# The mixture stage of a graph layer as seven half products, with the edge sums in a stage of their own

## The reference

```
gnn: h = xn @ W.T + b;  every node its own edge too;  out[row] += deg[row]^-0.5 deg[col]^-0.5 h[col]
mix: q = xn @ Wq.T + bq (k, v alike), 16 heads of 64;  q' = relu(q P) / 8, k' alike;  kv = k'^T v
     mix = (q' kv) @ Wo.T + bo
x = x + gnn + mix
ffn: routing weights over 8 experts;  sum_e w_e * (silu(y Wg_e) * (y Wu_e)) @ Wd_e,  y = layernorm(x)
x = x + ffn
```

## Time and profile before

| | |
|---|---|
| median of 3 runs | 1088.25 us (1088.06 to 1088.41) |
| the profiled execution | 1088.11 us, its span 1086.2 us |
| granted TensorE clock, mean | 0.998 |
| PE busy | 1075.5 us, 99%, 5587 matmuls |
| DVE, ACT, POOL busy | 441.6 us, 269.9 us, 323.0 us |
| from the last h tile to the router | about 549 to 758 us of the span |

### The profile page before, as it was taken

One profiled execution on the slowest core, in us unless ns is written; L12 is line 12 of the kernel. 1 busy time (PEld: TensorE's weight loads), 2 busy tenths in 40 slices (PEclk: granted clock), 3 DMA queues, 4 the chain that ended last, 5 costly groups with the idle time before them and its releaser, 6 DMA issues.

```text
span 1086.2 us, 15078 instructions
## 1 busy us (share of the span) xinstructions
PE 1075.5 (99%) x5587; PEld 893.3 (82%) x5587; DVE 441.6 (41%) x1061; ACT 269.9 (25%) x413; POOL 323.0 (30%) x223
## 2 busy tenths in 40 slices
PE   8999999999999999999999999999999999999998
PEld 7887778887878888888878888887788888888887
DVE  6944666676641111322212123344235112314684
ACT  5320211112233345311111112434213112202221
POOL 4000011122132347400035444434208744500151
PEclk9999999999999999999999999999999999999999
DMA  7313011122244487604179987876045646205912
GB/s 269 97 30 108 13 35 54 61 70 72 70 128 127 159 296 247 209 1 155 39 196 327 307 243 205 235 218 186 1 160 189 213 179 214 66 24 221 378 66 110
DMA packets 148731, 162.36 MB, mean 149 GB/s; under 512 B 8150, under 2 KB 116018, under 8 KB 145330
## 3 DMA queue, kind: packets, MB, share of 16 engines
q1 hardware_dynamic: 148082, 159.55, 45.5%
q10 hardware_dynamic: 576, 1.84, 0.4%
HBM read 114.91 MB, written 46.45 MB: 149 GB/s over the span
## 4 chain that ended last, share of the span: by engine, by line
PE 95%; DVE 3%; issue 1%; ACT 1%; DMA 0%; ACTq 0%; DVEq 0%
PE ps L1773 10%; PE ps L1774 9%; PE ps L1775 9%; PE ps L2073 7%; PE ps L2074 7%; PE ps L2075 7%; PE ps L2014 4%; PE ps L2008 4%; PE ps L1988 3%; PE ps L1989 3%; PE ps L1939 3%; PE ps L1990 3%; PE ps L1940 3%; PE ps L1941 3%; PE ps L2131 3%; PE ps L2132 3%
## 5 line engine op out<-in xcount | busy, mean ns | idle before, releaser
L1773 PE MATMUL ps<-w_hi,xnH 128*128 128x512 f32 x464 | 184.7, 398 | 0.0
L1775 PE MATMUL ps<-w_hi,xnL 128*128 128x512 f32 x464 | 180.9, 390 | 0.0
L1774 PE MATMUL ps<-w_lo,xnH 128*128 128x512 f32 x464 | 180.8, 390 | 0.0
L827 POOL TENSOR_TENSOR acc<-acc,cw 128x320 f32<-128x320 f32 x40 | 35.7, 892 | 252.6 <-ACT cw L1028 251.4
L1773 PEld LDWEIGHTS ps<-w_hi,xnH 128*128 128x128 f32 x464 | 87.1, 188 | 18.8
L1775 PEld LDWEIGHTS ps<-w_hi,xnL 128*128 128x128 f32 x464 | 87.1, 188 | 18.6
L1774 PEld LDWEIGHTS ps<-w_lo,xnH 128*128 128x128 f32 x464 | 87.2, 188 | 17.0
L1675 DVE TENSOR_TENSOR prd<-ps,wB 128x512 f32<-128x512 f32 (+1 forms) x24 | 14.2, 592 | 142.1 <-PE ps L2075 101.2
L1939 PE MATMUL ps<-xnH,w_hi 128*128 128x512 f32 (+1 forms) x192 | 68.1, 355 | 0.0
L2073 PE MATMUL ps<-x2H,guH 128*128 128x512 f32 (+1 forms) x192 | 67.7, 352 | 0.4 <-ACT wT L1232 0.4
L2074 PE MATMUL ps<-x2L,guH 128*128 128x512 f32 (+1 forms) x192 | 67.6, 352 | 0.0
(11 more groups left out here) (421 smaller groups left out, 2127.0 us busy)
## 6 DMA issues: line engine op xcount, KB each, us to landing
cR<-c_d SPq DMA_DIRECT2D x20, 640.0 KB, 5.2
foldin<-in SPq DMA_DIRECT2D x32, 256.0 KB, 2.8
guR<-in SPq DMA_DIRECT2D x16, 512.0 KB, 5.7
w_raw<-in SPq DMA_DIRECT2D x14, 512.0 KB, 6.4
c_d<-cw SPq DMA_DIRECT2D x40, 160.0 KB
wdq<-in SPq DMA_DIRECT2D x6, 1024.0 KB, 7.3
qs0H<-qT_d SPq DMA_DIRECT2D x10, 512.0 KB, 5.2
qs0L<-qT_d SPq DMA_DIRECT2D x10, 512.0 KB, 6.5
```

Source lines behind the costliest of these rows:

```text
L1773: pe.matmul(target, xnH[:, kc, cols], wH[w][:, kc, :], start=(kc == 0), stop=False)
L1774: pe.matmul(target, xnH[:, kc, cols], wL[w][:, kc, :], start=False, stop=False)
L1775: mm = pe.matmul(target, xnL[:, kc, cols], wH[w][:, kc, :], start=False, stop=(kc == KC - 1))
```

## The change

The mixture q' M is now made as the down projection is: M is cut into four blocks of 512 x 512, the tokens into two halves of five tiles, and seven products of combined halves take the place of eight. The 35 products (`seven_products(0, q, r)`, the old `down` made general by a stage number s) stand ahead of all 20 edge sums, which follow without a mixture between them. What goes with it:

- q' is stored as one float32 row set, not as two parts; a third store keeps M's raw blocks (`mr_d`), for which DVE copies them (`mR`).
- During the h stage M's blocks are combined in four rounds: SP loads four raw blocks, POOL makes four sums, ACT and POOL split each (`mix_high` in the h loop ahead of `h_high`), SP stores both parts (`mt_d`). In rounds 0 to 2 SP also loads the diagonal tiles of the counts, POOL adds the identity, SP stores them back (`own_counts`): the own nodes are counted once, and not at each load.
- The q rows stay in SBUF, loaded behind the last use of xn (`load_q`), and x1 is built up in the same place; it is stored for the end of the kernel, but no longer loaded back.
- The counts have six rooms and are loaded up to three tiles ahead. The bias of the output projection is added by DVE in the first half and by POOL for the second.
- PE's transposes, and with them `x2_hi` and `x2_low`, come one more tile later. ACT's `x2_hi(t - 3)` stands ahead of `ln2_sqrt(t)`, DVE's `x2_low(t - 3)` ahead of `add_sums`.

```diff
# SP, in the h stage and behind it
+            for k in range(3):
+                if k:
+                    sp.wait_ge(own_st, 64 * k)
+                own_counts(k, True)
+                load_mix_blocks(k)
+                own_counts(k, False)
+                for n in range(4 * k, 4 * k + 4):
+                    store_mix_block(n)
+            sp.wait_ge(*made(("h", 0, NT - 1)))
+            for q in range(2):
+                load_mix_panel(q)
+            load_mix_blocks(3)
+            for n in range(12, 16):
+                store_mix_block(n)
+                load_q(n - 12)
+            for t in range(4, NT):
+                load_q(t)
...
+            def load_mix_blocks(k):
+                if k:
+                    sp.wait_ge(wd_st[1], 64 * k)
+                for j, (h, g) in enumerate(((0, k), (1, k), (0, k + 4), (1, k + 4))):
+                    sp.dma_start(mixR[j][:], mr_d[h, :, g, :]).then_inc(in_d[0], 16)
...
# POOL, behind panel_lo(1)
+            for k in range(4):
+                if k < 3:
+                    pool.wait_ge(in_own, 16 * min(4 * k + 4, NT))
+                for t in range(4 * k, min(4 * k + 4, NT)):
+                    pool.tensor_tensor(own[:, t % 4, :], own[:, t % 4, :], ident[:], ALU.add).then_inc(c_own, 1)
+                pool.wait_ge(in_d[0], 64 * (k + 1))
...
+                    pool.tensor_tensor(mixR[target][:], mixR[first][:], mixR[second][:], op).then_inc(wd_mix, 1)
+                for n in range(4 * k, 4 * k + 4):
...
+                    pool.tensor_tensor(mixL[room_of][:], mixR[room_of][:], mixH[:].bitcast(F32), ALU.subtract)\
+                        .then_inc(wd_lo, 1)
...
# ACT, h stage
+            def mix_high(n):
+                act.wait_ge(wd_mix, 4 * (n // 4) + (1, 2, 4, 3)[n % 4])
+                if n:
+                    act.wait_ge(wd_lo, n)
+                    act.wait_ge(wd_st[0], 16 * n)
+                act.activation(mixH[:], mixR[MIX_MADE[n % 4][0]][:], ACT.Copy).then_inc(wd_hi, 1)
...
             for hf in range(2):
                 for t in range(NT):
                     if hf == 0 and t < 4:
                         panel_hi(1, t, 1)
+                    if 3 <= NT * hf + t < 19:
+                        mix_high(NT * hf + t - 3)
+                    if hf and t == NT - 1:
+                        token_high(0, 0)
+                        token_high(0, 1)
                     h_high(hf, t)
...
# token_high(0, i): for q = 0, 1, 4 it waits for the loaded q rows
+                if q in (0, 1, 4) and s == 0:
+                    act.wait_ge(in_q[q // 4], 32 * HALF)
...
# ACT, edge sums
             count_high(0)
+            count_high(1)
             for i in range(2 * NT):
                 t = i - NT
-                if i + 1 < 2 * NT:
-                    count_high(i + 1)
-                if t == NT - 1:
-                    ln2_sqrt(t)
-                if t >= 1:
-                    for h in range(2):
-                        x2_hi(t - 1, h)
-                if 0 <= t < NT - 1:
-                    ln2_sqrt(t)
-                if t >= 0:
-                    ln2_out(t)
+                if t >= 3:
+                    for h in range(2):
+                        x2_hi(t - 3, h)
+                if i + 2 < 2 * NT:
+                    count_high(i + 2)
+                if t >= 0:
+                    ln2_sqrt(t)
+                    ln2_out(t)
                 if t == NT - 2:
                     gu_high(0)
+            for t in (NT - 3, NT - 2):
+                for h in range(2):
+                    x2_hi(t, h)
...
# DVE, h stage and edge sums
             for hf in range(2):
                 for t in range(NT):
+                    if hf and t == NT - 1:
+                        token_low(0, 0)
+                        token_low(0, 1)
                     h_out(hf, t)
                     h_low(hf, t)
...
+            dve.wait_ge(in_q[1], 32 * HALF)
+            seven_products(0)
...
+            add_bias(0)
             for i in range(2 * NT):
                 t = i - NT
+                if t >= 3:
+                    x2_low(t - 3)
                 add_sums(i)
-                if i + 1 < 2 * NT:
-                    add_mixture(i + 1)
-                if 1 <= t < NT - 1:
-                    x2_low(t - 1)
+                if i + 1 < NT:
+                    add_bias(i + 1)
                 sum_stats(i)
                 if t >= 0:
                     ln2(t)
-                if t == NT - 1:
-                    x2_low(t - 1)
-            x2_low(NT - 1)
+            for t in range(NT - 3, NT):
+                x2_low(t)
...
# PE
             pe.wait_ge(*drained(("h", 1, NT - 1)))
-            mixture(0)
+            for q in range(7):
+                for r in range(HALF):
+                    seven_products(0, q, r)
             for i in range(2 * NT):
-                if i + 1 < 2 * NT:
-                    mixture(i + 1)
                 aggregate(i)
-                if i >= NT + 1:
-                    x2_transposes(i - NT - 1)
+                if i >= NT + 2:
+                    x2_transposes(i - NT - 2)
+            x2_transposes(NT - 2)
```

More of the change, by code:

```diff
@@ L372, in gps_layer @@
         c_lo = sem("c_lo")
[L373 to L375 removed]
+        x_in = [sem(f"x_in{hf}") for hf in range(2)]
         a_done = sem("a_done")
@@ new lines, in load_mix_panel, with load_q @@
+            def load_mix_panel(q):
+                blocks = slice(0 if q == 0 else 4, 4 if q == 0 else 8)
+                for part in range(2):
+                    source = mt_d[q - 2, part] if 2 <= q < 6 else m_d[q // 6, part, :, blocks, :]
+                    sp.dma_start((mwH, mwL)[part][q % 2][:].bitcast(F32), source).then_inc(in_w[0][2 * (q % 2) + part], 16)
+            def load_q(t):
+                sp.wait_ge(*made(("h", 1, t)))
+                cols = slice(t * P, (t + 1) * P)
+                for k in range(2):
+                    sp.dma_start(qR[k][:, :, cols], qT_d[4 * k:4 * k + 4, :, cols].rearrange("k q n -> q k n"))\
+                      .then_inc(in_q[t // HALF], 16)
@@ new lines, in seven_products @@
+            def seven_products(s, q, r):
+                i, target = q * HALF + r, down_bank(GROUP[q], r)
+                bank_is_free(s, q, r)
+                if r == 0 and s == 0:
+                    for part in range(2):
+                        pe.wait_ge(in_w[0][2 * (q % 2) + part], 48 + 16 * (q // 2 + 1))
+                elif r == 0 and q < 2:
+                    pe.wait_ge(wd_lo, 16 + 6 + q)
+                elif r == 0:
+                    pe.wait_ge(in_wd[min(q - 2, 2)], 32 if q < 4 else 96)
+                pe.wait_ge(hx_lo, 7 * HALF * s + i + 1)
+                opens = q not in (1, 4, 6)
+                panel_hi, panel_lo = seven_panel(s, q)
+                for k in range(4):
+                    hi, lo = hxH[s][i % 3][:, k, :], hxL[s][i % 3][:, k, :]
+                    high, low = panel_hi[:, k, :], panel_lo[:, k, :]
+                    pe.matmul(target, hi, high, start=(opens and k == 0), stop=False, skip_group_check=not opens)
+                    pe.matmul(target, hi, low, start=False, stop=False, skip_group_check=not opens)
+                    mm = pe.matmul(target, lo, high, start=False, stop=(k == 3), skip_group_check=not opens)
+                mm.then_inc(d_mm, 1)
```

639 lines of the change are left out of this document (320 added, 319 removed).

## The result

The changed kernel takes 1117.53 us (median of four runs, 1116.51 to 1118.39) against 1088.15 for the kernel before: a ratio of 1.027, 95% interval 1.025 to 1.029. The forecast, 1104.2, had the direction right; the time lies above the top of its range, 1111. The profiled execution has a span of 1114.7 us, 28.5 more than before.

The account below looks back on a forecast made before the run. PE, busy 99% of the 1086.2 us span, was taken as the bound. 1088.1 - 13.6 - 0.6 + 15.8 + 13.0 + 1.5 = 1104.2 us, slower by 1.5%; range 1089 to 1111.

Parts of the forecast that it names:

- Removed work: Mixture cut from 480 to 420 matmuls on PE, -13.6 us; wait ahead of the edge sums' transposes gone, -0.6 us.
- Term 1: Edge sums alone: DVE-ACT loop 6.63 us a tile against 5.42, gu's copies 1.9, late end 5.4; +15.8 us, bounds 12 and 18.
- The bias sums in the first half: First-half edge sums: DVE's bias sums beside POOL's count_low, at most 5.06 us a tile against PE's 4.53; taken as 0.
- Term 2: Entry to the mixture products: round 3's blocks behind panels, then q's loads, delay the start; +13.0 us, bounds 3.5 and 16.
- Term 3: Granted clock after the entry's gap: PE for a time at 1.2 GHz of 2.4; +1.5 us, bounds 0 and 3.
- Rival C: Second half of edge sums: 1.2 us gaps hold PE at 1.2 GHz, 29 us more, 1133 us; chance 0.05.

Follow-up runs that it names:

- the rooms apart: Changed kernel with another entry alone: a semaphore per mix room, POOL's first low part behind two sums, q and panel loads moved between stores; 1099.61 us, 1.011.
- the entry's order: Changed kernel with only SP's order changed: first panel in round 2, second behind all q loads, q's loads between a block's stores from block 8; 1109.60 us, 1.020.
- the edge sums' order: Changed kernel with only ACT's and DVE's order changed in the edge sums' second half: x2_hi ahead of ln2_out, x2_low behind ln2; 1107.21 us, 1.018.
- q left out: Version with all orders open, without the 20 loads of q; DVE sets q's tiles to zero instead; 1080.43 us, 0.993.
- all open: Changed kernel with separate mix rooms, edge sums reordered, tokens 0 and 1 behind last h tile, router(0) ahead, gu's copies behind two tiles; 1082.84 us, 0.9945.

## Why the prediction failed

- **Removed work, -13.6 and -0.6: right.** PE has 60 matmuls fewer, and no wait in the 35 products. The panels cost PE nothing there.
- **Term 1, +15.8: right.** The stage from the first product to the router took 3.7 us more. Take off the clock, 2.0 us at its start and 0.8 in the last transposes (783.2 to 784.8): 0.9, so term 1 measured 15.1, with the removed work as counted. Spacing (6.61), gu (1.9) and the end (5.4) came as worked out, and the changed order took the loop away.
- **The bias sums in the first half, 0: right.** All ten of DVE's sums of x1 rows and bob were slow beside POOL, 3.2 to 3.45 us; five of them in the answer on that line (ns min/median/max):

```profile
L1712 DVE TENSOR_TENSOR qR<-qR,bob x5: 3429/3441/3452, 693.3 to 711.8; 128x512 f32<-128x512 f32 x5
```

  A tile took DVE 4.6 us (the bound was 5.06) against 4.53 on PE. PE has no wait there, as the two banks took the rest up. The Trainium skill (SBUF — State Buffer, "Who interferes with whom") has two SBUF inputs on VectorE contend with GpSimd; the 3.44 us agrees.
- **Term 2, +13.0: the term that was mis-sized; it measured +23.3** (572.38 against 549.07), above its bound of 16. The chain was the right one; its steps were late one after another. Block 11 was to be copied at 519.2 and was at 524.3, 5.1 late: I let rounds 0 to 2 keep the slots of the h tiles, while a round, with four block loads behind the last low store and all four sums ahead of the first low part, takes 24 us of its own. Two rounds of 24.6 and 23.7, where four slots give 21.8 to each, are 4.7 of these 5.1 us; the rooms apart, which undo these two, ran rounds 0 and 1 in 22.1 and 20.8 and began round 2 at 506.5 instead of 512.0. From there to copy 12 I allowed 18.7 and it took 20.5: 1.8 more. Copies 12 to 15 were to take 12.6 and took 15.4, mostly because copy 14 waited 5.07 for a store between q's loads, which I had at 2.1 and about 1 for the loads: 2.8. From copy 15 to the start 11.5 became 12.2: 0.7. Together 10.4. That the panels held the blocks up was right; the move of the panels alone showed 9.7 us of it.
- **Term 3, +1.5: mis-sized.** I counted one fall. There are two that cost something: 2.0 us at the start and 2.4 at the router, 4.4 in all; a third, ahead of 552, lies before the long wait and costs nothing. At the router I had the wait (5.4 us) but no clock behind it. The bound of 3 was too low as well.
- The sum with these sizes: 1088.1 - 14.2 + 15.1 + 23.3 + 4.4 = 1116.7, where the profiled execution took 1116.5. Rival C, the second half at half clock, didn't come: six waits of 0.8 to 0.9 us (I had seven of about 1.2) left the clock at 1.00.

The range was too short above all because the bounds of term 2 varied only its last links (panels, q) and no bound stood for the rounds before them. With these 5.1 us its top would have been 1116, still short of 1117.5; the rest is copies 12 to 15 and the clock.

## What to carry to other kernels

Where helpers work in rounds beside a stage, work out a round's own cycle (last store, landing, loads, sums) and compare it with the time the stage gives it: a slot that is wide enough for a block doesn't mean that the round fits. A scheme that hides its helpers in one place is hidden there by the time between uses and by its neighbours; write the order anew where it gets less time, as two lines moved on ACT and DVE gave 10 us here. When PE loses its cover, the work that was hidden comes up as a chain, and a link that is freed gives back less than worked out for it, as the next one stands close behind: the entry's order gave 7.9 us where 15 or more were expected, the rooms 17.9 of 20 or more, and behind the opened edge loop stood the loads of counts.

## What the runs showed of the hardware that was not expected

- A second queue gave no shelter. With 1 MB loads issued on another queue 0.6 and 1.1 us ahead of a 256 KB store, ACT's wait for the store was 6.0 and 6.8 us, against 3.8 and 4.0 with the same loads 0.4 us behind the store on its own queue, and 1.9 to 2.0 without loads. The Trainium skill (DMA: Bandwidth & Descriptors, "Issuing engines are not separate DMA queues") says that DMAs of several issuing engines run on the same 16 DMA engines and interleave; the trace agrees. That the version with two queues was 4.6 us slower may be due to the order of issue.
- The clock: waits of 3.3 us (the edge sums' order), 4.0 (q left out), 4.7, 5.4, 6.2 (all open) and 16.8 were each followed by a granted clock of 0.50, 1.2 GHz; the waits of 0.8 to 0.9 us in six tiles, and one of 1.5 in all open, were not. Ahead of the wait of 5.4 there is one of 2.7 and 1.2 us of work; the clock was at 0.50 from 778.0 on, 0.1 us into the longer wait. The forecast knew of one such stretch only the earlier trace rows.
- A fall of the clock can cost less than it seems: filling the wait gave the full clock back and 0.8 us, which is within the noise, since the next late load stood right behind.
